# Value products of three self-attentions issued as two strip sets in a row, with 15 or 16 probability buffers

## The reference

```
s = jnp.einsum('bqhd,bkhd->bhqk', q, k) * scale      # L2: s = where(mask, s, min)
a = jax.nn.softmax(s, axis=-1)
o = jnp.einsum('bhqk,bkhd->bqhd', a, v)              # 'the value products'
```

## Time and profile before

| what | value |
| --- | --- |
| median of 3 runs | 2811.17 us (2807.91 to 2816.3) |
| profiled execution, span from first to last instruction | 2821.7 us (the page gives no other time of it) |
| PE busy | 2412.4 us, 85% |
| DVE busy | 1739.0 us, 62% |
| ACT busy | 1278.2 us, 45% |
| value products of `self2` of row 1 | first 1472.57 us, last 1868.18 us |
| value products of `self3` of row 0 | first 1932.38 us, last 2281.55 us |
| value products of `self3` of row 1 | first 2327.49 us, last 2586.52 us |

### The profile page before, as it was taken

The page is one execution under the profiler, slowest core; times in us unless marked ns, Lnnn a source line. Parts: engine busy times, 40 slices in busy tenths (PEclk is TensorE's granted clock), DMA queues, the critical chain, the costliest instruction groups (busy, mean ns, idle before and its releaser), DMA issues.

```text
span 2821.7 us, 37245 instructions
## 1 busy us (share of the span) xinstructions
PE 2412.4 (85%) x13127; PEld 1230.5 (44%) x13127; DVE 1739.0 (62%) x5398; ACT 1278.2 (45%) x2434; POOL 338.8 (12%) x350
## 2 busy tenths in 40 slices
PE   6678677978997979999878899988889989898887
PEld 2455334544554544554434445442234332223544
DVE  5555976665234675567766565657676677774443
ACT  2334444443221314455535555545646637665533
POOL 3001342243020100000200010000000010001011
PEclk8799788889998989999989999998999989999989
DMA  4566322000000120001411100133120032100110
GB/s 160 150 141 192 102 90 66 14 24 8 0 8 30 68 62 12 12 24 35 149 60 46 37 16 12 33 114 100 39 45 12 20 110 85 46 20 10 57 53 15
DMA packets 150926, 160.65 MB, mean 57 GB/s; under 512 B 33391, under 2 KB 120258, under 8 KB 150476
## 3 DMA queue, kind: packets, MB, share of 16 engines
q1 hardware_dynamic: 150740, 158.28, 19.8%
HBM read 97.39 MB, written 60.19 MB: 56 GB/s over the span
## 4 chain that ended last, share of the span: by engine, by line
PE 62%; DVE 19%; ACT 6%; DMA 5%; issue 5%; POOL 2%; SPq 1%; ACTq 0%; POOLq 0%; DVEq 0%
PE bank L1151 9%; PE bank L1710 8%; PE bank L1123 7%; PE bank L1098 7%; PE bank L1731 5%; PE bank L1127 3%; PE bank L756 3%; PE bank L1632 3%; DVE max L1224 3%; PE bank L2185 2%; DVE bank L1221 2%; PE bank L2362 2%; DVE k_stack L1418 1%; PE bank L683 1%; DVE stats L641 1%
## 5 line engine op out<-in xcount | busy, mean ns | idle before, releaser
L1165 ACT ACTIVATE work<-bank 128x512 f32<-128x512 f32 (+1 forms) x1216 | 698.7, 597 | 562.9 <-PE bank L1127 259.6
L1221 DVE CUSTOM_DVE_ANT_0 bank<-bank,weights 128x512 f32<-128x512 f32 x512 | 349.5, 702 | 186.3 <-PE bank L1098 184.8
L1098 PE MATMUL bank<-k_stack,q_stack 97*128 97x512 bf16 x896 | 362.4, 407 | 60.8 <-DVE max L1221 30.7
L1224 DVE TENSOR_REDUCE max<-bank 128x1 f32<-128x512 f32 x512 | 337.7, 685 | 123.6 <-PE bank L1098 121.4
L1123 PE MATMUL bank<-q_stack,k_stack 99*128 99x512 bf16 x896 | 347.8, 390 | 12.7 <-ACT work L1165 10.6
L1710 PE MATMUL bank<-hT,weights 128*128 128x512 f32 x512 | 265.4, 618 | 11.6 <-ACT work L1756 6.0
L1127 PEld LDWEIGHTS bank<-ident_b,weights 128*128 128x128 bf16 x2048 | 159.8, 98 | 120.1 <-issue 11.5
L1098 PEld LDWEIGHTS bank<-k_stack,q_stack 97*128 97x128 bf16 x896 | 89.5, 100 | 269.3 <-DVE max L1221 104.3
L1731 PE MATMUL bank<-weights,work 128*128 128x256 f32 x768 | 199.2, 386 | 5.9 <-DVE work L1791 5.8
L1127 PE MATMUL bank<-ident_b,weights 128*128 128x128 bf16 x2048 | 200.5, 220 | 0.0
L756 PE MATMUL bank<-hT,weights 128*128 128x512 f32 x288 | 160.7, 652 | 13.2 <-ACT hT L717 10.1
(11 more groups left out here) (242 smaller groups left out, 3587.0 us busy)
## 6 DMA issues: line engine op xcount, KB each, us to landing
q_stack<-parts_q SPq DMA_DIRECT2D x60, 384.0 KB, 3.8
parts_q<-parts SPq DMA_DIRECT2D x46, 384.0 KB, 2.6
k_stack<-parts_k SPq DMA_DIRECT2D x40, 384.0 KB, 4.9
weights<-parts_q SPq DMA_DIRECT2D x36, 384.0 KB, 3.7
parts_q<-parts SPq DMA_DIRECT2D x46, 256.0 KB, 2.9
parts_k<-parts SPq DMA_DIRECT2D x24, 384.0 KB, 2.6
parts_k<-parts SPq DMA_DIRECT2D x24, 256.0 KB, 2.9
weights<-in_L_e_w SPq DMA_DIRECT2D x12, 512.0 KB, 6.2
```

The costliest lines, as they stand in the source:

```text
L1098: m = pe.e.matmul(bank.ap[:, :], self.q(g)[0:MAX_ROW, h, qt * P:(qt + 1) * P], k_stacks[self.key, g].ap[0:MAX_ROW, h, half * BLK:(half + 1 ...
L1165: ac.e.activation(p.ap[0:self.nk, :], banks[self.key, "exp", g, i].ap[0:self.nk, :], ACT.Exp).then_inc(*probs.tick((self.key, g, i)))
L1221: ve.e.tensor_tensor_reduce(bank[:, :], bank[:, :], mask_bias[:, qt, half * BLK:(half + 1) * BLK], 1.0, -3.4e38, ALU.add, ALU.max, to).the ...
L1224: ve.e.tensor_reduce(to, bank[:, :], AX_X, ALU.max).then_inc(*maxima.tick((self.key, g, i)))
```

## The change

In `self2` of batch row 1 and in both `self3`, the value products are issued for two key blocks at a time: every 8 beats instead of every 4 (`sets=2`), at beats 50, 58, 66 and 74 of a group instead of 46, 50, ... 74. The products of key blocks 1, 3, 5 and 7 keep their beat, those of 0, 2, 4 and 6 come 4 beats later. Their number, their operands and their sums are the same. `self2` of batch row 0 is left alone.

A probability must now live longer, so there are more buffers for them: 16 in `self2` of row 1 and 15 in the two `self3`, of 512 columns each. The added ones are `work[17]` and `work[18]`, which lane d uses only in the experts of L1, two in the experts' `routed` array, and five (L2) or four (L3) in parts of the weights area that are not in use then. ACT waits, ahead of its first exp tile of such an attention, until those areas are no longer read (`more_free`). For that the weights area and `routed` are allocated ahead of `work`, which moves addresses in SBUF.

```
-        work = slots([sb(f"work{i}", [P, BLK]) for i in range(20)])
+        W = sb("weights", [P, 8192 + 15360])
+        wX, wY, wC = W[:, 0:4096], W[:, 4096:8192], W[:, 8192:8192 + 15360]
+        routed = sb("routed", [P, TPB, C])
+        routed_rows = routed[:, :, :].rearrange("p t c -> p (t c)")
+        spare = [routed_rows[:, i * BLK:(i + 1) * BLK] for i in range(2)]
+        spare += [wC[:, at:at + BLK] for at in (*range(2048, 4096, BLK), *range(10240, 12800, BLK))]
+        work = slots([sb(f"work{i}", [P, BLK]) for i in range(20)] + spare)
...
-                self.nprob = 7 if kind == "full" else 6
+                self.probs_at = lane.work[0:7 if kind == "full" else 6] + tuple(more_probs)
+                self.sum_at, self.more_free, self.sets = lane.work[7 if kind == "full" else 6], more_free, sets
...
                     if now := self.group(beat, self.pv_at, self.n):
-                        if now[1] % 4 == 0:
-                            self.pv(pe, now[0], now[1] // 4)
+                        if now[1] % (4 * self.sets) == 0:
+                            for at in range(self.sets):
+                                self.pv(pe, now[0], now[1] // 4 + at)
...
-                work.take(self.lane.work[n % self.nprob], (self.key, "prob", g, i), (pv_sums, (self.key, g, i)))
+                work.take(self.probs_at[n % len(self.probs_at)], (self.key, "prob", g, i), (pv_sums, (self.key, g, i)))
...
+                        for done, key in self.more_free if now == (0, 0) else ():
+                            ac.wait_ge(*done[key])
...
         full_of = dict(max_banks=(0, 1), exp_banks=(2, 3), pv_banks=(4,), lags=(32, 40, 46, 74))
+        paired_of = dict(full_of, lags=(32, 40, 50, 74), sets=2)
...
+            mask_left = [(exp_scores, (("L2", 1, "full", None), 7, 31)), (maxima, (("L2", 1, "full", None), 7, 31))]
+            experts_left = [(turned, (st["e", 1].key, "routed", 1)), (dense, (st["e", 1].key, "o", 2)), (dense, (st["e", 1].key, "all"))]
...
-                                    **full_of)
+                                    **(full_of, dict(paired_of, more_probs=(17, 18, 20, 21, 26, 27, 28, 29, 30), more_free=experts_left))[b])
...
-                                    period=32, stacks=(0, 1, 2), stacks_free=[(pool_done, ("third", 0))], **full_of)
+                                    period=32, stacks=(0, 1, 2), stacks_free=[(pool_done, ("third", 0))],
+                                    more_probs=(17, 18, 20, 21, 22, 23, 24, 25), more_free=mask_left, **paired_of)
```

More of the change, by code:

```diff
@@ L237, in build_program @@
         o_view = [hT[b][:, :, :, :].rearrange("p n c (t f) -> p (n c t) f", f=C) for b in range(B)]
-        W = sb("weights", [P, 8192 + 15360])
-        wX, wY, wC = W[:, 0:4096], W[:, 4096:8192], W[:, 8192:8192 + 15360]
         q_buf = [sb(f"q_stack{i}", [P, PAIR, S], BF16) for i in range(2)]
@@ L293, in build_program @@
         small = sb("small", [P, TPB, 8])
-        routed = sb("routed", [P, TPB, C])
         prow = sb("p_rows", [P, TPB, E])
@@ L987, in __init__ @@
             def __init__(self, lane, b, name, kind, q_parts, k_parts, v, v_ready, out_free, max_banks, exp_banks, pv_banks,
-                         period, lags, stacks, rows_ready, keys_ready, stacks_free=(), mask=False, lead=5, blk=None):
+                         period, lags, stacks, rows_ready, keys_ready, stacks_free=(), mask=False, lead=5, blk=None,
+                         more_probs=(), more_free=(), sets=1):
                 self.lane, self.b, self.name, self.kind, self.mask, self.lead = lane, b, name, kind, mask, lead
@@ L1133, in pv @@
                     bank = banks.take(self.bank("pv", g), (self.key, "pv", g), (evac, (self.key, "sum", g)))
-                    work.take(self.lane.work[self.nprob], (self.key, "sum", g), (turned, (self.key, "sum", g)))
+                    work.take(self.sum_at, (self.key, "sum", g), (turned, (self.key, "sum", g)))
                     for f in bank.free:
```

## The result

The kernel with the change takes 2829.59 us in the median of 13 runs (2816.21 to 2835.92), the kernel before 2816.23 in 13 runs beside it (2807.91 to 2825.49). The ratio is 1.0041, with a 95% interval of 1.0025 to 1.0057. The prediction was 2799.1, faster; it is slower, and the time is outside the range of 2788 to 2816.

The account below looks back on a forecast made before the run. The prediction took PE to bound most of the kernel. It summed -4.1 us in PE-bound stretches and -8.0 us for the remaining pairs to -12.1 us, from 2811.2 to 2799.1 us, with an 8-in-10 range of 2788 to 2816.

Parts of the forecast that it names:

- The price of the switch: On PE, joining two sets of value products saves 0.21 us per pair, at most 20.2 us over 96 pairs.
- The drained join: On PE, the second set waits for the first, starting after 1.05 us: 4 us saved at best, 2807; chance 0.04.
- The PE-bound stretches: Three stretches where lane d's MLP or output projection fills PE: 19.5 pairs gain 0.21 us each, 4.1 us.
- The edits at nothing: Buffers, copy at a group's end, bank 4, `more_free` waits, DMAs and addresses: each taken to cost nothing.
- the other 76.5 pairs: Pairs outside the stretches that PE fills: between -16.1 and +4.6 us; half of the gain taken, 8.0 us.
- a purely DVE-bound pair gains nothing and loses 0.06: In the rhythm without lane d, eight tiles take 6.64 us with joined sets against 6.58 before.
- Lane d's chains come late: Where lane d passes between PE, ACT and DVE, every third of 76.5 pairs pays 0.87 us: +10.1, 2821.3; chance 0.09.
- The clock falls: In DVE-bound runs of 8 tiles, half clock costs about 6 pairs some 4 us each: 2823 us; chance 0.03.
- The longer hole eats it: Pairs outside the PE-bound stretches lose 0.06 us each: +0.5 us in all, 2811.7 us; chance 0.20.
- The test set for it: Prediction wrong if the granted clock in the three attentions' windows falls below 0.99, 0.96 and 0.99.
- Its own tests: Wrong if PE's waits for DVE's maxima grow over 8 us, or those ahead of L1104, L964, L683 by some 12.
- The reading before it: PE, busy 91% of the three attentions' 1004.2 us, ends last over most of the program.

Follow-up runs that it names:

- buffers-only kernel: The change's 15 or 16 buffers, new waits and addresses, but single sets at their old beats, against the kernel before: 0.9997.
- two beats apart: Second set of each pair two score tiles behind the first, against the kernel before: both `self3` 1.0019; only `self3` row 1, with `self2` row 1 joined, 0.9961.
- one-attention kernels: Pairs in one attention each, against the kernel before: `self2` of row 1 0.9983, `self3` of row 0 1.0044, `self3` of row 1 1.0019.

## Why the prediction was wrong

**What held.** *The price of the switch.* A pair on PE, after:
```profile
1952.53 1.91 PE L1157 MATMUL bank<-work,v 128*17 128x512 f32 x16
...
1954.37 0.39 PE L1104 MATMUL bank<-weights 97*128 97x512 bf16 x1
```
From its start to the next instruction it is 1.84 us, against 0.87 + 0.98 = 1.85 worked out, and its 16 matmuls cover 1.91, against 0.87 + 1.05 = 1.92. The second start itself shows where the two sets read different buffers, as in the kernel with pairs in row 1:
```profile
2387.76 1.05 PE L1157 MATMUL bank<-weights 128*17 128x512 f32 x8
2388.63 1.04 PE L1157 MATMUL bank<-work,weights 128*17 128x512 f32 x8
```
It comes 0.87 us behind the first, on the same bank. The drained join (a second start at 1.05) is false, and so, for this join, is the rule that it came from: "TensorE: Matmul & The Clock Gate", Part 3 of the Trainium skill, by which weight loads overlap with matmuls in flight only where the row groups differ. The same skill's "TensorEngine Tiling (Array Packing)", Key Properties, says that a change of tiling mode drains TensorE; the trace agrees in so far as a change costs time, 0.09 us in and 0.12 out.

*The PE-bound stretches.* Lane d's MLP beside `self2` of row 1, 8 pairs, before and after:
```profile
1671.10:1787.30 116.20, 115.34 (x709) 62.42 (x711) 68.94 (x175) 64.68 (x112) 4.15 (x4) 1.00 0.06 15
1663.90:1778.10 114.20, 113.40 (x707) 63.16 (x706) 68.70 (x175) 64.73 (x112) 4.20 (x4) 1.00 0.06 15
```
That is 2.0 us less, 0.25 per pair (0.21 worked out). But of the 1.9 us for the 9 pairs of the MLP stretch of `self3` row 0 only 0.6 arrived:
```profile
2111.40:2218.80 107.40, 107.36 (x487) 50.73 (x490) 72.31 (x118) 71.00 (x124) 6.89 (x8) 1.00 0.04 8
2113.40:2220.20 106.80, 105.41 (x483) 52.01 (x481) 72.05 (x118) 71.07 (x124) 6.16 (x7) 1.00 0.03 8
```
PE's own work fell by the whole 1.95 us, and PE, which had not been idle at all, now was for 1.4.

*The edits at nothing.* No exp waits for a set; the only waiter for L1157 is still the copy of the sums, 60.3 us in 38 waits for 39.6 in 35:
```profile
  ACT work L960: 60.3, 38
```
The copy waits 20.7 us longer, against the 21 that it named; that this cost nothing no run isolates. The buffers-only kernel at 0.9997 bears out the zeros for buffers, addresses and `more_free`.

**The step that failed** is the bound of the other 76.5 pairs, "a purely DVE-bound pair gains nothing and loses 0.06", used as the worst that the hole can do, with half of the gain taken as the value. The working behind it added up one long idle time against two short ones, and its own numbers are right (1.67 us measured). It assumed that every one of the short holes had been paid for in full, and that nothing else lands in the long one. Neither holds: of the 42 waits in row 1 with single sets, 15 were of 0.63 us or less, so joining two sets gave back less than the long hole added, and where lane d's own set follows a pair the hole is 2.9 us. In `self3` of row 1, at a full clock, a pair cost +0.18 to +0.25 us. The term for these pairs was -8.0 us; its upper end was +4.6. In the profiled execution of after it came to about -5 in `self2` (-7.2 less the 2.0 of the MLP stretch), +13 in `self3` of row 0 (+12.2 and the 0.6 of its MLP stretch) and +5 in `self3` of row 1.

The same step took one rhythm for all 76.5 pairs, that of `self3`, where PE issues a max tile and an exp tile in 0.45 us and DVE needs 0.62. In `self2` the mask adds four matmuls to each exp tile. Its rhythm in before, from set to set without lane d:
```profile
1479.26 1.05 PE L1151 MATMUL bank<-work,weights 128*17 128x512 f32 x8
1480.24 0.39 PE L1098 MATMUL bank<-k_stack,q_stack 97*128 97x512 bf16 x1
...
1480.91 0.38 PE L1098 MATMUL bank<-k_stack,q_stack 97*128 97x512 bf16 x1
...
1483.03 1.05 PE L1151 MATMUL bank<-work,weights 128*17 128x512 f32 x8
```
PE takes 0.67 us per beat, and DVE, where it works from a full bank, starts its maxima 0.61 to 0.64 apart. So PE does not catch up with DVE, and two sets of 3.77 us are 7.54. The first two pairs of after start 7.38 apart (1476.68 and 1484.06) with 0.15 of a cross tile between them, so 7.23. The 16 pairs ahead of the MLP gained, before and after:
```profile
1472.10:1671.10 199.00, 174.24 (x1384) 86.97 (x1383) 132.19 (x402) 107.37 (x186) 7.21 (x9) 0.97 0.16 44
1470.70:1663.90 193.20, 171.46 (x1383) 87.55 (x1381) 130.63 (x401) 106.60 (x186) 7.01 (x9) 0.97 0.17 45
```
In the three other kernels with pairs here this stretch took 193.2 to 195.0 us (clock 0.96 or 0.97), in ten with single sets 195.1 to 203.4 (198.6 to 201.0 in the seven at clock 0.97). In the 81 us behind the MLP pairs lost 0.4. That the mask is what makes the difference is read from the rhythm; no kernel without it was run.

**"Lane d's chains come late"**, with a chance of 0.09, was nearest in mechanism and near in size (+10.1 us, where 0.41% is 11.6). It put the price at 0.87 us for every third pair. What the traces show is lane d's cross tiles waiting up to 3.3 us for 1.7, and three sets in a row where lane d's own set follows a pair. It named DVE's division as the place; that was not where time went: in the stretch of 64 us PE's wait for it went from 8.3 to 8.9 us, in the same 5 waits.

**"The clock falls"**, 0.03, most likely took part, but not as told: not in runs of score tiles where DVE is the bound (row 1 has them, and stayed at 1.00 in the kernel with pairs there alone), but in the first two groups of `self3` row 0, among lane d's cross tiles. That its +11.9 us is so near the measured 11.6 is luck. That the long hole itself brings the clock down is likely, since four executions with pairs were all lower there than seven with single sets, but no run isolates it. The test set for it, a clock below 0.96 in the second window, came true (0.93). It read the 0.81 of the earlier trace rows as that of a run of max tiles, but that is a mean: to 2300 us lane d's matmuls stand between them and the clock is 1.00, and where max tiles are alone but for one transpose it is 0.50:
```profile
2310.00:2320.00 10.00, 5.41 (x10) 0.92 (x9) 9.48 (x36) 0.00 (x0) 0.00 (x0) 0.50 0.00 1
```
**"The longer hole eats it"**, at 2811.7, had the right mechanism and too small a price.

**Its own tests.** PE's wait for DVE's maxima (L1098, now L1104) was to grow by over 8 us if the prediction is wrong. It fell, from 30.5 + 32.9 + 46.8 = 110.2 to 18.7 + 27.2 + 51.4 = 97.3 us, and so did the waits for others ahead of L1104, L964 and L683 together, from some 84 to 71 us. That watched the wrong side of the hand-over: the harm was DVE waiting for PE. In the stretch of 64 us that is 17.2 to 26.8 us.

**The reading before it.** PE 91% busy was taken as near to PE-bound. But PE was busy for 88% of the stretch of `self2` that gained, and for 93% and 90% of the two of `self3` row 1 that lost: the busy share does not tell them apart. In the places that lost, DVE and PE wait for each other in turns, and 3.2 us less of PE's work in the three windows (914.2 to 911.0) came with 13 us more of PE's idle time.

**Open.** How much of the loss in row 0 is the clock; why two beats apart gains in one stretch only; what PE waits for in the MLP stretch of row 0, which gave 0.6 us and not 1.9; why the 16 pairs ahead of the MLP of `self2` gave over 5 us, more than 16 x 0.21.

## What to carry over

Joining work on one engine to save a switch pays where that engine, tile for tile, is the slower side of the hand-over or has other work to fill its waits (here `self2`, 0.67 us against 0.64, and the MLP stretch beside it). Where it is the faster side (here `self3`, 0.45 against 0.62), weigh the saving per join (0.2 us) against the extra time that the engines fed through two buffers then stand idle (0.86 us for a plain hole, 1.67 less 0.81), and count a cover that is already there as lost. The busy share of a long window does not say which case it is. Read each stretch on its own and change only those that gain (here one attention of three), and look for what lands behind the longer block in the same beat, such as another lane's set. As the test of such a change watch the wait of the fed engine for the feeder, not the other way round.

## What the runs showed of the hardware

The four column strips of a second set start before the first set's second passes end by the trace's modelled ends, on the same strips and the same bank: 16 matmuls of 512 float32 columns in 1.91 us, for 1.05 of a set of 8. A join between banks and one within a bank cost the same: the second set starts 0.87 us behind the first in both.

The granted clock differs from run to run of one kernel, and its time with it. Over 32 runs of the kernel before beside the one-attention kernels (2811.09 to 2831.5 us), a straight line through time against mean clock falls by 1549 us per 1.0. One us at half clock lowers the mean by 0.5/2820, so it goes with 0.27 us of time. This is a relation among runs, not a cause that was tested. The mean clock of the 13 runs of after was 0.9232, of those 32 of before 0.9263; they were timed in different sets of runs, so what follows is rough: by that line 4.8 of the 11.6 us (0.41%) of loss go with the clock, where the estimate from single stretches gave 5 of 9.
